# Storing every output tile by itself, in the order of the results, and reloading a batch three steps behind its first result

## What is computed

```
def _gn(v, G=32, eps=1e-05):
    g = v.reshape(B_, G, C_ // G, H_, W_)
    m = jnp.mean(g, axis=(2, 3, 4), keepdims=True)
    s = jnp.var(g, axis=(2, 3, 4), keepdims=True)
    return ((g - m) / jnp.sqrt(s + eps)).reshape(v.shape)

x = x + _L0_conv_ref(_gn(x), L0_conv_offset)
x = x + _L1_conv_ref(_gn(x))
```

## Time and profile before

| what | value |
|---|---|
| median of 3 runs | 257.6 us (256.43 to 259.06) |
| the profiled execution | 258.49 us |
| its span, first to last instruction | 256.7 us |
| VectorE busy | 197.5 us, 77% |
| TensorE matmul busy | 163.9 us, 64% |
| ScalarE busy | 136.2 us, 53% |
| GpSimd busy | 38.7 us, 15% |
| moved by DMA | 76.79 MB, mean 299 GB/s |

### The profile page before, as it was taken

How to read it: one execution, slowest core, us unless ns; L and a number is a source line. 1 busy time by engine, 2 the same in 40 slices (tenths; PEclk the granted TensorE clock), 3 DMA queues, 4 the chain that set the end, 5 groups by cost and what they waited for, 6 DMA issues and landing times.

```text
span 256.7 us, 2406 instructions
## 1 busy us (share of the span) xinstructions
PE 163.9 (64%) x664; PEld 94.4 (37%) x664; DVE 197.5 (77%) x321; ACT 136.2 (53%) x217; POOL 38.7 (15%) x39
## 2 busy tenths in 40 slices
PE   0000000607986969758896696999999999989610
PEld 0000000407735639658853422444433333333200
DVE  0799999999973179855850348999999999999930
ACT  1000999679762056315210499898887877870000
POOL 0000000000000052100104782000705370000000
PEclk9999999999996599997999577999999999999965
DMA  5999999999999308999971657239999999997798
GB/s 166 416 411 409 409 409 290 363 410 409 409 306 258 80 2 235 337 273 279 269 169 22 173 189 259 84 92 368 349 325 412 402 416 406 403 410 320 278 407 344
DMA packets 26223, 76.79 MB, mean 299 GB/s; under 512 B 7969, under 2 KB 8225, under 8 KB 25921
## 3 DMA queue, kind: packets, MB, share of 16 engines
q1 hardware_dynamic: 19616, 67.12, 71.9%
q0 software_dynamic: 4752, 9.45, 12.0%
q10 hardware_dynamic: 1840, 0.06, 0.5%
HBM read 67.07 MB, written 29.99 MB: 378 GB/s over the span
## 4 chain that ended last, share of the span: by engine, by line
DVE 39%; DMA 33%; SPq 10%; PE 7%; ACT 3%; issue 2%; ACTq 0%; DVEq 0%
DMA ring<-x_pad 27%; DVE ring L959 21%; DVE parts L273 10%; PE ps L570 3%; DMA blk<-x_pad 3%; SPq L291 2%; PE ps L659 2%; SPq L310 2%; SPq L292 2%; DMA stat_rows<-blk_stat 2%; ACT blk L534 2%; DVE blk L273 2%; PE ps L589 1%; ACT parts L542 1%; SPq L303 1%
## 5 line engine op out<-in xcount | busy, mean ns | idle before, releaser
L659 PE MATMUL ps<-parts,had_sb 128*128 128x512 f16 x216 | 55.1, 391 | 8.0 <-DVE parts L273 5.7
L959 DVE SCALAR_TENSOR_TENSOR ring<-ps,beta,ring 128x1024 f32<-128x1024 f32 x48 | 59.8, 1280 | 0.4 <-PE ps L659 0.4
L579 PE MATMUL ps<-geo_sb,blk 128*128 128x128 f32 x72 | 12.0, 320 | 51.9 <-DMA blk<-x_pad 45.4
L823 DVE BATCH_NORM_STATS2 halfstat<-ring 128x6 f32<-128x512 f32 x64 | 38.8, 673 | 1.9 <-DMA ring<-x_pad 1.8
L589 PE MATMUL ps<-parts 128*128 128x160 f32 (+2 forms) x180 | 31.2, 336 | 11.8 <-ACT parts L464 10.2
L534 ACT ACTIVATE blk<-ring,gn 128x1024 f32<-128x1024 f32 x32 | 37.8, 1227 | 0.0
L273 DVE TENSOR_TENSOR parts<-blk,parts 128x1024 f16<-128x1024 f32 x27 | 32.9, 1219 | 6.0 <-ACT parts L542 6.0
L285 POOL DMA_INDIRECT ring<-x_rows,row_at x24 | 29.7, 1237 | 50.8 <-DMA ring<-x_pad 38.5
L659 PEld LDWEIGHTS ps<-parts,had_sb 128*128 128x128 f16 x216 | 20.4, 100 | 44.2 <-issue 11.2
L589 PEld LDWEIGHTS ps<-parts 128*128 128x128 f32 x180 | 29.8, 214 | 13.1 <-ACT parts L464 10.6
L669 PE MATMUL ps<-ring,first_w 128*128 128x512 f32 x64 | 32.3, 628 | 0.0
(11 more groups left out here) (117 smaller groups left out, 146.6 us busy)
## 6 DMA issues: line engine op xcount, KB each, us to landing
ring<-x_pad SPq DMA_DIRECT2D x20, 1536.0 KB, 15.3
out<-ring SPq DMA_DIRECT2D x13, 1536.0 KB, 7.4
blk<-x_pad SPq DMA_DIRECT2D x15, 512.0 KB, 17.1
out<-ring SPq DMA_DIRECT2D x9, 512.0 KB, 5.1
x_rows<-blk POOLq DMA_DIRECT2D x6, 512.0 KB, 6.9
other_a<-x_pad SPq DMA_DIRECT2D x2, 512.0 KB, 8.3
x_rows<-other_a POOLq DMA_DIRECT2D x2, 512.0 KB, 6.1
geo_sb<-geo SPq DMA_DIRECT2D x1, 683.0 KB, 4.8
```

Of the source, the lines that this page charges most:

```text
L579: last = pe.transpose(pixels[:, j // 4, 128 * (j % 4):128 * (j % 4 + 1)], shifted[:, 128 * j:128 * (j + 1)], eye)
L659: last = pe.matmul(ps[n % 4][:, h, :], had_sb[:, sign, :], part_of(n, t, part)[:, 512 * h:512 * (h + 1)], start=False, stop=ends and part ...
L823: last = dve.bn_stats(halfstat[:, i % 4, t, h, :], ring[:, t, place_of(i), 512 * h:512 * (h + 1)])
L959: dve.scalar_tensor_tensor(ring[:, m, place_of(i), :], ps[n % 4][:, :, :].rearrange("p a n -> p (a n)"), beta[:, i % BATCH:i % BATCH + 1], ...
```

## The change

It is in SP's program alone. `BY_TILE` goes. `store(n, t)` stores one tile, after its own result and nothing else, and is called in VectorE's order of results, in steps n = 0 to 17: tile 2 of batch n, tile 0 of batch n - 1, tile 1 of batch n - 2. The waits for the store two before are gone. The stores of batches n = 0 to 3 each have a semaphore of their own, all others share `last_stores`. `reload(n - 3)` stands at the end of steps n = 3 to 6, behind the three stores of that step.

```
-BY_TILE = (0, BATCH - 2, BATCH - 1)
...
-        store_done = [sem(f"store_done{u}") for u in range(2)]
+        store_done = [sem(f"store_done{n}") for n in range(EXTRA)]
+        last_stores = sem("last_stores")
...
-            def stored(n):
-
-                return 16 * sum(CT if i in BY_TILE else 1 for i in range(n % 2, n + 1, 2))
-
-            def store(n):
+            def store(n, t):
+
                 i = n + EXTRA
+                sp.wait_ge(result_done[t], n + 1)
+                signal = store_done[n] if n < EXTRA else last_stores
+                sp.dma_start(out_v[i % BATCH][:, t, :], ring[:, t, place_of(i), :]).then_inc(signal, 16)
+
+            def reload(j):
+                sp.wait_ge(store_done[j], 16 * CT)
+                sp.dma_start(ring[:, :, j, :], x_bcp[j]).then_inc(reload_done[j], 16)
+
+            for n in range(BATCH + 2):
+                if n < BATCH:
+                    store(n, 2)
+                if 1 <= n <= BATCH:
+                    store(n - 1, 0)
                 if n >= 2:
-                    sp.wait_ge(store_done[n % 2], stored(n - 2))
-                if n in BY_TILE:
-                    for t in (2, 0, 1):
-                        sp.wait_ge(result_done[t], n + 1)
-                        sp.dma_start(out_v[i % BATCH][:, t, :], ring[:, t, place_of(i), :]).then_inc(store_done[n % 2], 16)
-                else:
-                    for t in (2, 0, 1):
-                        sp.wait_ge(result_done[t], n + 1)
-                    sp.dma_start(out_v[i % BATCH], ring[:, :, place_of(i), :]).then_inc(store_done[n % 2], 16)
-
-            def reload(j):
-                sp.wait_ge(store_done[j % 2], stored(j))
-                sp.dma_start(ring[:, :, j, :], x_bcp[j]).then_inc(reload_done[j], 16)
-
-            for n in range(BATCH):
-                if n in (1, EXTRA):
-                    reload(n - 1)
-                store(n)
-                if 1 < n < EXTRA:
-                    reload(n - 1)
-            for n in range(BATCH - 2, BATCH):
-                sp.wait_ge(store_done[n % 2], stored(n))
+                    store(n - 2, 1)
+                if 3 <= n < 3 + EXTRA:
+                    reload(n - 3)
+            sp.wait_ge(last_stores, 16 * CT * (BATCH - EXTRA))
```

## The result

The changed kernel took 249.72 us (median of 6 runs, 247.98 to 251.97) against 256.97 us before (6 runs, 255.74 to 259.06). The ratio is 0.9735, with a 95% interval of 0.9691 to 0.9779. So the change takes 2.3 to 2.7% off, 5.9 to 6.8 us. The forecast was 6.5 us, and 251.1 us as the time.

A forecast was written before the change was run, and what follows sets the result against it. VectorE's chain of results, then DMA draining 12 tiles behind it, set the end; eight tiles from 238.0 us at 1.30 us plus 1.8 us give a 250.2 us span, 6.5 us less, so 251.1 us from the median, range 249.5 to 254.5 us.

The forecast's parts named there:

- Bytes that could have gone at 232 to 243 us go behind the last result: Kernel before, near the end: DMA partly empty while VectorE is full, then DMA at 0.94 for ten more microseconds.
- Issues cost nothing: SP's queue: 26 more issues, at the dearest 3.8 us per step of 5.84 us, costed at nothing.
- Term 1: Ahead of 175 us: five tiles, 2.6 MB of stores, move into idle DMA time; 0.5 MB of reload moves back.
- Term 2: From 175 us: 24.3 MB at 392 GB/s are gone at 236.9 us, about 1 us before the last eight results begin.
- Term 3: Tail from 238.0 us: eight tiles at 1.30 us each plus 1.8 us end at 250.2 us, 6.5 us less.
- term "1.8 us": End of the span: start of the first transfer, landing of the last and end of the program take 1.8 us.
- The reload chain: Reloads and gathers ahead of ACT's batch 15: ACT does not wait, cost nothing; rival that it comes late, chance 0.02.
- I expect part 7 within 2 us of where it was: Fourth reloaded batch, gathered for ACT's batch 15: arrives within 2 us of before, when it had 7.7 us of slack.
- It costs one for one behind 226.3 us: Late-reload rival: ACT and VectorE wait for the fourth reloaded batch, a loss when it lands behind 235 us; chance 0.02.
- Small transfers do not overlap: Slower rival, in the tail: 2.6 us per tile store, span 260.6 us, 3.9 us slower; chance 0.04.
- the milder form of 2.1 us a tile: No-change rival, in the tail: tile stores drain slower than whole ones, tail ends at 256.6 us; chance 0.05.
- A backlog at 238 us: Half-gain rival: DMA queue not empty when the last eight results begin; at 3 us, gain 3.5 us; chance 0.13.

The follow-up runs named there:

- early_only: Changed kernel up to batch 11, then as the kernel before: batches 12 and 13 stored whole, 14 and 15 as three tiles each; 255.27 us, ratio 0.9982.
- tail_only: Kernel before up to batch 11; only batches 12 to 15 stored tile by tile in VectorE's order of results; 254.69 us, ratio 0.9809.
- change_again: The changed kernel, unaltered, profiled and timed once more; 249.91 us, ratio 0.9769 to the kernel before.
- reload_4: Changed kernel with the four reloads one step later; 252.47 us, ratio 0.9802 to the kernel before.
- pool_both: Changed kernel with GpSimd making tile 2's low part for six batches and issuing the four reloads in place of SP; 250.43 us, ratio 0.9764.
- size_clean: Kernel before with each whole store issued as three 512 KB stores, only after all three results of the batch; 256.5 us, ratio 0.9928.
- pool_low: Changed kernel with the low fp16 part of tile 2 made by GpSimd instead of VectorE for six batches; 248.1 us, ratio 0.9637.
- whole_no_waits: Changed kernel storing whole batches after their third result, without waits for an earlier store; 255.67 us, ratio 0.9979.
- size_only: Kernel before with every whole store issued as three tile stores, each waiting for its own result alone; 254.55 us, ratio 0.9933.
- reload_2: Changed kernel with the four reloads one step earlier; 259.38 us, ratio 1.0106 to the kernel before.

## Why the prediction was right, step by step

**Where the bytes go.** "Bytes that could have gone at 232 to 243 us go behind the last result": right; `early_only` keeps that hole and keeps the time.

**Issues cost nothing.** Right. One issue took 0.33 us at the median, 1.63 us at most, with the queue full behind it.

**Term 1, five tiles early.** Right: q1 moved 3.83 MB from 150 to 171 us (2.10 MB before), 1.7 MB more where the sum had 2.1 MB, and 28.86 MB were left from 171 us on, where the sum had 28.5 MB. `tail_only` shows its price if left out, 2.3 to 3.2 us.

**Term 2, the queue is just empty.** Right, with more room than reckoned. The full stretch ran at a mean of 395 GB/s (392 assumed) and the holes of 228 to 236 us, share 0.78, are 1.8 us of spare time.

**Term 3, the tail.** The sum had 8 x 1.30 us and 1.8 us behind (13, 0), 12.2 us. In `change_again` (13, 0) exists at 235.0 us and the span ends at 247.3 us, 12.3 us. In the first profile it is 234.1 to 247.3 us, 13.2 us. The 1.0 us too much is at the very end. Stretches of half a microsecond, in the kernel before and in the changed kernel:

```profile
255.20:255.70 0.50, 0.00 (x0) 0.00 (x0) 0.00 (x0) 0.00 (x0) 0.00 (x0) 0.50 0.98 393
255.70:256.20 0.50, 0.00 (x0) 0.00 (x0) 0.00 (x0) 0.00 (x0) 0.00 (x0) 0.50 0.08 25
```
```profile
244.80:245.30 0.50, 0.00 (x0) 0.00 (x0) 0.00 (x0) 0.00 (x0) 0.00 (x0) 0.65 1.01 393
245.30:245.80 0.50, 0.00 (x0) 0.00 (x0) 0.00 (x0) 0.00 (x0) 0.00 (x0) 0.50 0.07 25
245.80:246.30 0.50, 0.00 (x0) 0.00 (x0) 0.00 (x0) 0.00 (x0) 0.00 (x0) 0.50 0.06 25
246.30:246.80 0.50, 0.00 (x0) 0.00 (x0) 0.00 (x0) 0.00 (x0) 0.00 (x0) 0.50 0.02 8
```

A share of 0.06 is as much as one engine of 16. So about one DMA engine was 1 us behind the others, and the last store has landed only when its slowest engine is done. The term "1.8 us" was read from a tail in which all 16 ended together (share 0.98, then 0.08); it is a lower bound. The part of the tail with a full queue fell from 9.3 us (246.4 to 255.7 us) to 2.8 us in the first profile (242.5 to 245.3 us) and 2.9 us in the second, by 6.5 and 6.4 us: that is the forecast of 6.5 us. What the sum left out is the uneven end, which takes 1.0 us of it back in one profile and nothing in the other.

**The reload chain.** "I expect part 7 within 2 us of where it was": this step failed, and its failure was hidden. The fourth reload landed 13.7 us after its issue at 193.6 us; POOL's last gather and ACT's start of batch 15 in the changed kernel:

```profile
211.97 1.93 POOL L283 DMA_INDIRECT ring<-x_rows,row_at  x1 [0.30 <-issue]
```
```profile
222.40 0.40 ACT L516 ACTIVATE first_w<-geo_sb,gn 128x128 f32<-128x128 f32 x1 [1.29 <-PE ps L649]
```

With 9.0 us of landing the part came at 221.0 us, 1.4 us ahead of its use (about 3 us in `change_again`), where 7.7 us were left before. The sum let the queue grow at a mean rate, and had SP wait for (3, 1) for 2 us; it was 4.1 us, and the slices of the first reloads ran at 244 to 331 GB/s. So 5 to 6 us of slack were spent, and no time shows it. That some was left is luck: the sum had 5.7 us or more.

**"It costs one for one behind 226.3 us"** was wrong as well: in `reload_4` ACT came 2.1 us late and VectorE did not wait at all. The first microseconds of such a delay go into ACT's lead; in `pool_both`, where ACT waited 12.6 us, VectorE waited too.

**The rivals.** "Small transfers do not overlap", and the milder form of 2.1 us a tile: `size_clean` rules them out. Of the Trainium skill's rule of 1 MiB a transfer (DMA: Bandwidth & Descriptors, section Bandwidth) the trace shows the limits: with several 512 KB stores queued one behind the other the engines ran at 408 GB/s, as with whole ones (409 GB/s). The 2.0 us plus the bytes at 436 GB/s that the Trainium skill gives (same page, section Anatomy of one DMA) is a fit to transfers that GpSimd issues; a lone tile store of SP took 2.6 us to land, not the 3.2 us of that estimate. A backlog at 238 us did not come in the change; it came in `tail_only`, where the queue is full until 5.0 us behind the last result, against 2.8 us in the change. The loss that I did not list is the nearest one: the same stores with the reload one step earlier, 1% slower than before. The sentence on the waits of a reload ("the last of them issued one step earlier") held the reason why the change escapes it, but gave it no price.

## What to carry to other kernels

Store a piece as soon as it exists, in the order in which pieces come into being, if the DMA engines have idle time that late bytes could use; look for that time right ahead of the last results, and count the bytes that must leave behind the last of them. Early stores and a better order in the tail are worth their full sum only together, because either the last results or the bytes in all are the bound. On an in-order issuing queue never wait for the transfer issued last: put as much work between a transfer and the wait for it as keeps the DMA engines busy until it has landed.

## What the runs showed of the hardware

The 16 DMA engines do not always end together. In the kernel before the share falls from 0.98 to 0.08 from one half microsecond to the next. In `reload_4` it takes over two microseconds, with few bytes moved:

```profile
247.00:247.50 0.50, 0.00 (x0) 0.00 (x0) 0.00 (x0) 0.00 (x0) 0.00 (x0) 0.50 0.99 393
247.50:248.00 0.50, 0.00 (x0) 0.00 (x0) 0.00 (x0) 0.00 (x0) 0.00 (x0) 0.50 0.38 148
248.00:248.50 0.50, 0.00 (x0) 0.00 (x0) 0.00 (x0) 0.00 (x0) 0.00 (x0) 0.50 0.20 82
...
249.00:249.50 0.50, 0.00 (x0) 0.00 (x0) 0.00 (x0) 0.00 (x0) 0.00 (x0) 0.50 0.10 41
```

and in `pool_low`, with a queue that was full for some 65 us, over three:

```profile
240.00:244.00 4.00, 0.00 (x0) 0.00 (x0) 0.63 (x1) 0.00 (x0) 0.00 (x0) 0.90 1.00 401
244.00:248.00 4.00, 0.00 (x0) 0.00 (x0) 0.00 (x0) 0.00 (x0) 0.00 (x0) 0.50 0.15 60
```

Take the time from the end of the full queue to the end of the span. It is about 1.0 us in the seven profiles in which the engines had a clear hole ahead of the last of the bytes (a share of 0.31 or less over one to four microseconds between 230 and 240 us): both of the kernel before, `size_clean`, `early_only`, `whole_no_waits`, `change_again` and `pool_both`. It is 1.8 to 3.8 us in the five in which the queue had no hole, or hardly one (0.84 at the lowest for a microsecond between 228 and 240 us): `size_only`, `tail_only`, `reload_2`, `reload_4` and `pool_low`. The first profile of the change is the exception, with 2.0 us behind a hole of one microsecond at 0.26. This fits engines that drift apart while the queue never runs empty, but no run varied that by itself, and which engine lags, and why, stays open.
